# Projections of a fused delta-rule attention and expert kernel: float32 products made of float16 parts

## The reference

```
xn = layernorm(x)
q, k, v, g = xn@Wq, xn@Wk, xn@Wv, xn@Wg        # 4 heads, 128 wide (q, k), 64 wide (v, g)
beta = sigmoid(xn@Wb);  k = k * rsqrt(sum(k*k) + 1e-12);  q = q * 128**-0.5
S = S + k_t (beta_t (v_t - k_t^T S))^T;  o_t = q_t^T S      # a recurrence over 2048 tokens
s = (o * rsqrt(mean(o*o) + 1e-5) * norm_w * silu(g)) @ Wo
e(t) = argmax(xn@router_w)                     # one of 8 experts for each token
y = relu(xn@fc[e])**2 @ proj[e]                # 1024 hidden units
out = x + s * silu(y)
```

## Time and profile before

| | |
|---|---|
| median of 3 runs | 793.43 us |
| span of the profiled execution, first to last instruction | 792.3 us |
| PE / PEld busy | 765.0 us (97%) / 647.4 us (82%) |
| DVE, POOL, ACT busy | 528.3 (67%), 390.1 (49%), 348.8 (44%) us |
| chain that ended last | PE 80%, DVE 8%, issue 5%, POOL 5% |

### The profile page before, as it was taken

One profiled execution on the slowest core, in us unless ns is written; L12 is line 12 of the kernel. 1 busy time (PEld: TensorE's weight loads), 2 busy tenths in 40 slices (PEclk: granted clock), 3 DMA queues, 4 the chain that ended last, 5 costly groups with the idle time before them and its releaser, 6 DMA issues.

```text
span 792.3 us, 22185 instructions
## 1 busy us (share of the span) xinstructions
PE 765.0 (97%) x8994; PEld 647.4 (82%) x8994; DVE 528.3 (67%) x1153; ACT 348.8 (44%) x760; POOL 390.1 (49%) x407
## 2 busy tenths in 40 slices
PE   6979999999999999999999999999999999999986
PEld 5957988888888888888888887888788887879853
DVE  6695465575655657456575667777777767677788
ACT  4813534454444543445344453443444444435432
POOL 3815363553635436354363545546463645445351
PEclk9999999999999999999999999999999999999999
DMA  9508932533336333263333632404142323322076
GB/s 301 191 28 335 330 142 114 195 141 146 128 115 221 135 125 127 115 236 125 121 127 119 235 116 79 163 17 182 51 135 107 128 108 128 129 108 94 30 225 221
DMA packets 37748, 116.25 MB, mean 147 GB/s; under 512 B 3664, under 2 KB 24400, under 8 KB 27664
## 3 DMA queue, kind: packets, MB, share of 16 engines
q1 hardware_dynamic: 33904, 104.62, 36.1%
q0 software_dynamic: 3744, 10.23, 3.9%
HBM read 101.33 MB, written 13.50 MB: 145 GB/s over the span
## 4 chain that ended last, share of the span: by engine, by line
PE 80%; DVE 8%; issue 5%; POOL 5%; DMA 1%; another core or an unknown queue 0%; ACT 0%; DVEq 0%; POOLq 0%; SPq 0%
PE bank L504 18%; PE bank L515 15%; PE bank L548 7%; PE bank L533 6%; PE bank L580 5%; PE bank L480 4%; PE bank L478 3%; PE bank L479 3%; PE bank L620 2%; PE bank L638 2%; PE bank L629 2%; PE bank L722 2%; POOL XTl L2396 2%; PE bank L560 2%; POOL ImM L2416 2%
## 5 line engine op out<-in xcount | busy, mean ns | idle before, releaser
L515 PE MATMUL bank<-wts,hT 128*128 128x256 f32 x624 | 170.9, 393 | 0.0
L504 PE MATMUL bank<-xsT,wts 128*128 128x128 f32 x1248 | 166.0, 281 | 0.4 <-ACT xsT L1152 0.3
L504 PEld LDWEIGHTS bank<-xsT,wts 128*128 128x128 f32 x1248 | 150.5, 192 | 11.2 <-issue 11.1
L1757 DVE TENSOR_TENSOR Pm<-bank,lvl_mask 128x256 f16<-128x256 f32 x180 | 68.3, 419 | 68.5 <-PE bank L620 65.1
L515 PEld LDWEIGHTS bank<-wts,hT 128*128 128x128 f32 x624 | 105.4, 191 | 7.3
L2396 POOL TENSOR_TENSOR XTl<-f_t,XTh 128x512 f16<-128x512 f32 x32 | 39.9, 1254 | 138.4 <-DVE XTh L1697 138.3
L1768 DVE TENSOR_TENSOR M<-bank,M 128x256 f16<-128x256 f32 x180 | 68.9, 419 | 52.9 <-PE bank L629 52.1
L1198 ACT CAST Z<-bank 128x256 f16<-128x256 f32 x180 | 59.4, 376 | 99.8 <-PE bank L638 99.7
L1143 ACT ACTIVATE hT<-bank 128x512 f32<-128x512 f32 x78 | 46.7, 599 | 46.8 <-PE bank L504 46.7
L548 PE MATMUL bank<-xT,wq_sb 128*128 128x128 f32 x512 | 63.2, 277 | 0.4 <-DVE qT16l L1702 0.4
L580 PE MATMUL bank<-wvg_sb,xT 128*128 128x512 f32 x128 | 62.7, 612 | 0.0
(11 more groups left out here) (247 smaller groups left out, 1951.2 us busy)
## 6 DMA issues: line engine op xcount, KB each, us to landing
wts<-in_fc SPq DMA_DIRECT2D x39, 1024.0 KB
wts<-in_pj SPq DMA_DIRECT2D x39, 1024.0 KB
wts<-in_x SPq DMA_DIRECT2D x10, 512.0 KB, 7.1
wts<-y_d SPq DMA_DIRECT2D x4, 1024.0 KB, 9.1
out_x<-wts SPq DMA_DIRECT2D x16, 256.0 KB, 2.2
xn_d<-wts SPq DMA_DIRECT2D x3, 1024.0 KB, 5.0
x_first<-in_x SPq DMA_DIRECT2D x4, 512.0 KB, 17.5
wts<-in_x SPq DMA_DIRECT2D x4, 256.0 KB, 3.6
```

Of the source, the lines that this page charges most:

```text
L504: ins = pe.matmul(psum[bank[n]][:, (c % 4) * P:(c % 4 + 1) * P], fcw[r][:, k, c * P:(c + 1) * P], xsT[:, k, :], start=(k == 0), stop=(k == ...
L515: ins = pe.matmul(psum[bank[0]][:, 0:D], hT[:, c, :], pjw[r][:, c, :], start=(c == 0), stop=(c == HC - 1))
L1757: dve.tensor_tensor(h4(Pms[last(m)], b).rearrange("p h (n c) -> p h n c", c=s), half4(level_bank(m, b)).rearrange("p h (n c) -> p h n c", ...
```

## The change

`xT` becomes a float16 tensor with a high and a low part. ACT writes the high part out of the transposes' bank (`keep_xT`, now counting `xTh_ok`), and a new `xT_low(c)` on DVE subtracts it from the bank and writes the low part, counting `xT_ok`. The weights are loaded as float32 into the space that later holds `x_first`; `w_high(name)` on ACT multiplies them by 64 in place and copies them to float16, `w_low(name)` on POOL subtracts and writes the low part. Each product of a projection and of the logits is three float16 products (high x high, high x low, low x high) into the same bank. The factor 64 is taken out where q, v, the gate and beta leave their banks. Semaphores of the end are reused ones, since the count is limited, and SP waits for the last `w_low` before it loads `x_first`.

```diff
+W_SCALE = 64.0
+TERMS = [(0, 0), (0, 1), (1, 0)]
-        xT = sb("xT", [P, NCH, B, KC, P])
+        xT = sb("xT", [P, NCH, 2, B, KC, P], F16)
+        wk16 = sb("wk16", [P, 2, KC, H * DK], F16)
...
                 def K(a, b):
                     fr = At(pe, a)
                     if a == 0:
-                        pe.wait_ge(wk_in, 16)
+                        pe.wait_ge(wl_ok, W_ORDER["wk"])
                     pe.wait_ge(xT_ok, a + 1)
                     fr.on(P32_ok[b], back=1)
                     for k in range(KC):
-                        ins = pe.matmul(psum[KG_BANK[b]][:], xT[:, a, b, k, :], wk_sb[:, k, :],
-                                        start=(k == 0), stop=(k == KC - 1))
+                        for zx, zw in TERMS:
+                            ins = pe.matmul(psum[KG_BANK[b]][:], xT[:, a, zx, b, k, :], wk16[:, zw, k, :],
+                                            start=(k == 0 and zx + zw == 0), stop=(k == KC - 1 and zx == 1))
...
                 def keep_xT(c):
                     act.wait_ge(xnTp, c + 1)
-                    act.copy(xT[:, c].rearrange("p b k n -> p (b k n)"), psum[TR_BANK[c % 3]][:]).then_inc(xT_ok, 1)
+                    act.copy(xT[:, c, 0].rearrange("p b k n -> p (b k n)"), psum[TR_BANK[c % 3]][:]).then_inc(xTh_ok, 1)
+
+                def w_high(name):
+                    of, to = w_of[name]
+                    act.wait_ge(w_in[name], 16)
+                    act.activation(of, of, ACT.Copy, scale=W_SCALE).then_inc(wh_ok, 1)
+                    act.wait_ge(wh_ok, 2 * W_ORDER[name] - 1)
+                    act.copy(to[:, 0], of).then_inc(wh_ok, 1)
...
+                def xT_low(c):
+                    dve.wait_ge(xTh_ok, c + 1)
+                    dve.tensor_tensor(xT[:, c, 1].rearrange("p b k n -> p (b k n)"), psum[TR_BANK[c % 3]][:],
+                                      xT[:, c, 0].rearrange("p b k n -> p (b k n)"), ALU.subtract).then_inc(xT_ok, 1)
...
+                def w_low(name):
+                    of, to = w_of[name]
+                    pool.wait_ge(wh_ok, 2 * W_ORDER[name])
+                    pool.tensor_tensor(to[:, 1], of, to[:, 0], ALU.subtract).then_inc(wl_ok, 1)
...
                 def ramp():            # on ACT
+                    w_high("wbr")
+                    w_high("wk")
                     normal(0)
                     normal(1)
                     keep_xT(0)
                     normal(2)
                     keep_xT(1)
                     normal(3)
+                    w_high("wq")
                     ksq_(0, 1)
                     ksq_(0, 0)
...
                 def q_l(a, b):
                     fr = At(dve, a)
                     fr.on(qh_ok[b])
-                    dve.tensor_tensor(h4(qT16[1][a % 2], b), bank4(QV_BANK), h4(qT16[0][a % 2], b),
-                                      ALU.subtract).then_inc(ql_ok[b], 1)
+                    dve.scalar_tensor_tensor(out=h4(qT16[1][a % 2], b), in0=bank4(QV_BANK), scalar=1 / W_SCALE,
+                                             in1=h4(qT16[0][a % 2], b), op0=ALU.mult, op1=ALU.subtract).then_inc(ql_ok[b], 1)
```

More of the change, by code:

```diff
@@ L203, in build_program @@
         x_first = sb("x_first", [P, NCH // 2, B * D])
+        stage = x_first[:].rearrange("p c n -> p (c n)")
+        w_of = {}
+        for n, (name, t) in enumerate((("wk", wk16), ("wq", wq16), ("wvg", wvg16), ("wbr", wbr16))):
+            size = KC * t.shape[3]
+            w_of[name] = (stage[:, 1024 * n:1024 * n + size].rearrange("p (k n) -> p k n", k=KC), t)
         x_last = wts[:, 0:2 * W].rearrange("p (c n) -> p c n", c=NCH // 2)
@@ L547, in Q @@
                         for k in range(KC):
-                            ins = pe.matmul(bank4(QV_BANK)[:, h, :], wq_sb[:, k, h * DK:(h + 1) * DK],
-                                            xT[:, a, b, k, :], start=(k == 0), stop=(k == KC - 1))
+                            for zx, zw in TERMS:
+                                ins = pe.matmul(bank4(QV_BANK)[:, h, :], wq16[:, zw, k, h * DK:(h + 1) * DK],
+                                                xT[:, a, zx, b, k, :], start=(k == 0 and zx + zw == 0),
+                                                stop=(k == KC - 1 and zx == 1))
                     ins.then_inc(Qp[b], 1)
@@ L579, in VG @@
                     for k in range(KC):
-                        ins = pe.matmul(psum[QV_BANK][:], xT[:, a, b, k, :], wvg_sb[:, k, :],
-                                        start=(k == 0), stop=(k == KC - 1))
+                        for zx, zw in TERMS:
+                            ins = pe.matmul(psum[QV_BANK][:], xT[:, a, zx, b, k, :], wvg16[:, zw, k, :],
+                                            start=(k == 0 and zx + zw == 0), stop=(k == KC - 1 and zx == 1))
                     ins.then_inc(VGp[b], 1)
@@ L1180, in q_h @@
                     fr.on(Op, back=2)
-                    act.copy(h4(qT16[0][a % 2], b), bank4(QV_BANK)).then_inc(qh_ok[b], 1)
+                    act.activation(h4(qT16[0][a % 2], b), bank4(QV_BANK), ACT.Copy, scale=1 / W_SCALE).then_inc(qh_ok[b], 1)
                 def sig(a, b):
@@ L1252, in ramp @@
                     keep_xT(9)
+                    w_high("wvg")
                     keep_xT(10)
@@ L1850, in ramp @@
                     normal(1)
+                    xT_low(0)
+                    xT_low(1)
                     stats_of(2, 0)
@@ L1853, in ramp @@
                     stats_of(2, 1)
+                    xT_low(2)
                     variance(2)
+                    xT_low(3)
                     stats_of(3, 0)
@@ L2443, in ramp @@
                     k_l(0, 0)
+                    w_low("wvg")
                     route_consts()
```

107 lines of the change are left out of this document (68 added, 39 removed).

## The result

Device time fell from 794.2 us (median of four executions, 793.3 to 795.3) to 784.3 us (782.1 to 786.2): a ratio of 0.9874, interval 0.986 to 0.9887. The forecast was 785 us. The profiled execution has a span of 782.3 us, where the sum had 784.3. Of all executions behind this document one, of the second root first, took 1471.8 us; its cause is not known, and it bears on no number here.

What follows compares the result with a forecast made beforehand. PE, busy 765.0 of 792.3 us, was taken as the bound, with an equally long POOL-then-DVE path from `F` to `M0`. Span 792.3 + 14.7 - 0.5 - 20.5 - 1.7 = 784.3, plus 1.1: 785 us; range 771 to 797.

Steps and rivals of the forecast that it cites:

- PE's costs: On PE: six K matmuls 1.29 us, twenty-four of Q 1.34, logits 0.25 a chunk gained; 2.94 us gained per step.
- Rival (B): Every K, VG and Q: float16 weight loads show at 98 ns each, slowing the kernel to 825 us; chance 0.03.
- the 81 ns: The Trainium skill's gap between 128-column matmuls in a real stream; by it Q costs 1.94 us, 0.15 more than before.
- Steps of three: Loop: 1.47 us ahead of `M0` lost to waiting, 1.47 behind it kept; seven steps gain 10.3 us.
- All seven steps of three show this pattern: From `F` to `M0`, a POOL then DVE path exactly as long as PE's, in all seven steps of three.
- Rival (A): Whole kernel: PE is all that counts, giving 757 us, or 767 with the ramp as forecast; chance under 773: 0.08.
- Steps of two: Steps 9 to 12: of 1.47 us ahead of `M0`, 0.7 kept; 2.17 gained per step, 8.7 in all.
- The loop: Steps of three, step 8 and steps of two together gain 20.5 us; bounds 35 and about 10.
- The tail: Chunks 14 and 15: worth 5.9 us on PE, 1.7 kept because `M0(13)` and `M0(14)` wait for DVE.
- Rival (C): Ramp and loop: ramp costs 20 us while the loop gains only 10, giving 802 us; chance 0.13.
- The ramp: Start-up: splitting work on DVE, ACT and POOL moves `M0(0)` from 43.94 to near 58.6, +14.7 us; bounds +5 and +20.
- so all the rest moves with it: After `M0(0)`: routing and first expert weights follow DVE, so everything later shifts by +14.7 us, less 0.5 for one VG.

Runs made afterwards that it cites:

- second root first: Changed kernel, ACT normalising chunks 0 to 3 before splitting the key weights, POOL taking the second root before their low part: 786.0 us, ratio 0.9896.
- PT first: POOL's low parts of PT moved ahead of root, product and scatters in each step: changed kernel 771.6 us (0.9704), kernel before 790.8 us (0.9951).
- masks early: Changed kernel, POOL's routing and level masks moved into ramp pauses, DVE's two f_t ahead of chunk 8's low part: 784.2 us, ratio 0.9865.

## Why the prediction was right, and where it was not

**PE's costs** held: 1.30 for K (1.29), 1.34 for Q (1.34), 0.63 a chunk of logits. Rival (B), bare weight loads, is excluded, and with it the 81 ns that the prediction quotes: 24 matmuls of 128 columns took 56 ns each.

**Steps of three** held in both halves from step 2 on: nothing of 1.47 ahead of `M0`, 1.43 of 1.47 behind it. The reason is shown too: one order on POOL turned the wait of 1.64 us into 0.44 and gave most of the loop's gain back. In what remains DVE leads alone: from the copy at 403.81 to the end of the last `Z` at 407.52 it works without a pause, and `M0` follows at 407.57. Rival (A), PE alone, fell with it: a kernel with 43 us less on PE won 10. "All seven steps of three show this pattern" was wrong for step 1: there PE waited for `Z` before as after (0.76 and 0.89 us), and `F(0)` to `M0(1)` still lost 1.34. There DVE's copy of M followed `U` and not POOL: it started 12.27 us behind `F(0)` before and 10.64 after, and POOL's one low part of PT, 11.8 us behind `F(0)` in both, held one of the two copies for less than 1 us. So what PE gained ahead of `U` was kept.

**Steps of two** gained 2.35 where 2.17 was forecast. The 1.30 ahead of `M0` instead of 0.70 is mostly a matter of where one reads: `M0`'s first half starts earlier, and 0.47 of wait now stands between its halves. The reserve was 0.2 larger than read.

**The loop** with the step into it made 22.7 us (1.34 and 21.4) where the sum had 20.5: 1.3 of the difference is step 1, 0.7 the steps of two, 0.4 the way from `F(12)` to `M0(13)`, less 0.2 in the other steps of three. The tail made 3.4 where the sum had 1.7: `M0(13)` to `M0(14)` alone gave 1.8. Rival (C), a loop that gains 10 and a ramp that costs 20, came in neither half.

**The ramp** is the term that was mis-sized: 16.0 us at `F(0)`, forecast 14.2. Up to `M0(0)` the chain ran as forecast: statistics at 17.5 (17.0), `f_t` at 39.97 (40.1), k_l's end at 44.7 (44.8), masks' end at 56.0 (55.3), the copy of M at 55.05. `M0(0)` started at 56.45 and not at 58.6, but with its first half only; the second waited for DVE until 58.69. The routing's first reduction on DVE, behind the second `Zo`, moved from 44.13 to 58.53: 14.4 us, where the sum had 14.7.

The step that failed comes behind that: "so all the rest moves with it". It moved by more. Starts of the same pieces, before and after (us):

```
routing's first reduction, DVE      44.13 -> 58.53   +14.40
first rank matmul, PE               46.51 -> 61.76   +15.25
behind the 31 rank matmuls, PE      48.48 -> 64.37   +15.89
first gathered rows turned, PE      69.82 -> 85.54   +15.72
first expert tile, PE               70.81 -> 87.33   +16.52
F(0), PE                            97.20 -> 113.25  +16.05
```

The first 0.85 is one DVE instruction of 1.26 us for 0.42, which now runs beside POOL's low part of X (58.98 to 60.41):

```profile
45.02 0.42 DVE L1602 TENSOR_TENSOR wts<-wts,prefer 128x256 f32<-128x256 f32 x1
```

```profile
59.43 1.26 DVE L1628 TENSOR_TENSOR wts<-wts,prefer 128x256 f32<-128x256 f32 x1
```

The next 0.6 is the granted clock, which was 0.50 from 59.7 to 63.1: the rank matmuls took 2.52 us for 1.94. At the first expert tile PE then waited 1.12 us for the expert's weights, which landed 9.2 us after their issue; before, no such wait stood there. One VG behind it gave 0.5 back, as forecast. That these three come from the change, and would come in each execution, is not shown: there is one trace of each kernel.

The errors of ramp (-1.8) and of loop and tail (+3.9) have opposite signs, and the 785 is better than its parts. It is also better than its sum: the span came 2.0 us lower than the 784.3 of the sum, and the 1.1 us from span to time were 1.75 in the profiled execution (784.05 and 782.3). Both are luck.

Above all the sum could not tell what the 14.4 us up to the routing are made of. The prediction explained 5.2 of them by a root that waits for the key weights. Taking that wait away moved the statistics and nothing behind them. How they divide between the work added and its order on POOL and DVE stays open; the clock has no part in them in this execution, where it was full from 11.9 to 59.7.

## What to carry to other kernels

Read the gain of a faster stretch at the wait that ends it: here a cut ahead of a second path of equal length was worth nothing, the same cut behind it was worth all of itself, and moving two independent instructions on the other path's engine was worth more than the change. After such a change look again for what became the bound, since the edit that freed 13 us here was worth 4 before. A wait in a start-up chain is not a term that can be subtracted: put away here, it uncovered the next on the same queue.

## What the runs showed of the hardware

An engine that is relieved can lose its clock. The kernel before had PE busy 42 of the first 50 us at full clock; the changed one 31. Between 10 and 110 us the kernel before had the full clock throughout; the changed one had a granted clock of 0.50 for 6.8 us (from 59.7 and from 76.7), and the kernels built from it for 6.8 to 23.9. It is not relief alone: the kernel before with PT first, whose PE does the same work, had 3.4 us of it too, from 61.3. In several of these kernels the same instructions took up to twice as long there, behind idle places of 1.8 to 4.2 us: K(0) 5.1 to 5.3 us for 2.75, the first expert tile 4.05 for 2.50. Not each idle place does it (the changed kernel's Q(0,1) ran at full clock behind 3.18 us), nor is it the same in each execution: the two kernels with masks early, with and without PT first, do not differ up to the first expert tile, and one had 0.50 there and the other 1.00. Behind `M0(14)`, where PE waits 2.0 us, the stretch to `M0(15)` took 26.1 us in the changed kernel and 27.7 with masks early. PE from 700 to 705 us in the two (us, busy, granted clock, DMA share, GB/s):

```profile
700.00:705.00 5.00, 3.15 (x67) 1.00 0.00 0
```

```profile
700.00:705.00 5.00, 3.14 (x47) 0.80 0.00 0
```

Two such places of 1.6 us each make up most of the spread of the changed kernel's own executions, 782.1 to 786.2, in size; differences of 1 us between the ramps can't be told from it.
